# A four-slot graph network on one core: next inputs loaded early, and a new stage order on every engine

## What is computed

```
layer 0: A = exp(8*tanh((x q)(x k)^T / sqrt(128) / 8)) * adj, rows normalised; out = A x v
layer 1: x_h = elu(x Wi + bi); e = sigmoid(tgt_i + src_j + be) * mask; agg = e x_h
         out = [elu([agg, x_h * rowsum(e)] Wn + bn), x_h] Wm + bm
layer 2: Chebyshev terms I, L, 2LL-I of the normalised Laplacian; relu(sum_k T_k x W_k + b)
layer 3: 5 steps of a gated recurrence h -> (1-z)h + z*tanh(...), with adj*h in each gate
```

## Time and profile before

| | us |
|---|---|
| median of 3 runs | 2195.31 (2191.51 to 2196.2) |
| profiled execution, span | 2194.4 |
| VectorE busy | 1709.0 (78%) |
| ScalarE busy | 1182.5 (54%) |
| GpSimd busy | 1027.3 (47%) |
| mean granted TensorE clock | 0.952 of 2.4 GHz |

### The profile page before, as it was taken

One profiled execution on the slowest core, in us unless ns is written; L12 is line 12 of the kernel. 1 busy time (PEld: TensorE's weight loads), 2 busy tenths in 40 slices (PEclk: granted clock), 3 DMA queues, 4 the chain that ended last, 5 costly groups with the idle time before them and its releaser, 6 DMA issues.

```text
span 2194.4 us, 26908 instructions
## 1 busy us (share of the span) xinstructions
PE 1938.3 (88%) x8891; PEld 1418.6 (65%) x8891; DVE 1709.0 (78%) x3821; ACT 1182.5 (54%) x2177; POOL 1027.3 (47%) x812
## 2 busy tenths in 40 slices
...
GB/s 64 1 1 1 1 39 0 1 1 1 40 0 1 1 1 40 0 1 0 1 40 1 1 1 1 39 1 1 1 14 27 1 1 1 21 20 1 1 1 20
DMA packets 13512, 21.29 MB, mean 10 GB/s; under 512 B 2720, under 2 KB 5024, under 8 KB 13216
## 3 DMA queue, kind: packets, MB, share of 16 engines
...
q10 hardware_dynamic: 2576, 0.53, 0.1%
...
## 4 chain that ended last, share of the span: by engine, by line
PE 47%; DVE 29%; POOL 7%; ACT 7%; issue 6%; DMA 2%; SPq 0%; POOLq 0%; DVEq 0%; ACTq 0%
DVE X L696 5%; PE psA L1063 5%; PE psA L1064 5%; PE psB L890 4%; PE psB L892 3%; PE psB L891 3%; PE psA L885 3%; DVE H L848 3%; PE psA L1093 3%; DVE E L752 3%; DVE stat L675 3%; DVE E L844 2%; PE psA L890 2%; POOL rstd L390 2%; PE psA L891 2%
## 5 line engine op out<-in xcount | busy, mean ns | idle before, releaser
L425 POOL TENSOR_TENSOR S<-S,H 128x512 f32<-128x512 f32 x160 | 215.8, 1349 | 489.1 <-ACT S L562 489.1
L1063 PE MATMUL psA<-adjT_hi,nh_hi 128*128 128x512 f32 x640 | 273.7, 428 | 0.0
L1064 PE MATMUL psA<-adjT_hi,nh_lo 128*128 128x512 f32 x640 | 260.5, 407 | 0.0
L420 POOL TENSOR_TENSOR xT_lo<-H,xT_hi 128x512 fp32r<-128x512 f32 x160 | 240.4, 1510 | 32.8 <-ACT xT_hi L570 22.0
L381 POOL TENSOR_TENSOR S<-E 128x1024 f32<-128x1024 f32 x64 | 152.8, 2388 | 172.3 <-DVE E L710 119.1
L696 DVE TENSOR_SCALAR X<-X,mv,rstd 128x128 f32<-128x128 f32 x512 | 214.6, 482 | 16.2 <-POOL rstd L390 16.2
L388 POOL TENSOR_TENSOR rstd<-mv,eps_cols 128x4 f32<-128x4 f32 x128 | 49.3, 385 | 378.0 <-DVE mv L689 378.0
L844 DVE SCALAR_TENSOR_TENSOR E<-E 128x512 f32<-128x512 f32 x160 | 148.9, 931 | 95.3 <-ACT E L566 94.7
L665 DVE TENSOR_TENSOR nh_lo<-psA,nh_hi 128x512 fp32r<-128x512 f32 x128 | 88.0, 687 | 137.1 <-ACT nh_hi L575 137.1
L848 DVE SCALAR_TENSOR_TENSOR H<-E,S 128x512 f32<-128x512 f32 x160 | 165.2, 1032 | 9.3
L1093 PE MATMUL psA<-E,u5T 128*128 128x512 f32 x320 | 165.6, 599 | 0.0
...
## 6 DMA issues: line engine op xcount, KB each, us to landing
...
```

Source lines behind the costliest of these rows:

```text
L420: nc.gpsimd.tensor_tensor(xT_lo[s][:, :], H[s][:, :], xT_hi[s][:, :].bitcast(F32), ALU.subtract).then_inc(pool_done[s], 1)
L425: nc.gpsimd.tensor_tensor(kept[s], kept[s], H[s][:, :], ALU.mult).then_inc(pool_done[s], 1)
L1063: nc.tensor.matmul(psA[s][:, :], hi, adjT_hi[:, m, :], start=(m == 0), stop=False)
L1064: last = nc.tensor.matmul(psA[s][:, :], lo, adjT_hi[:, m, :], start=False, stop=(exact and m == TILES - 1))
```

## The change

The table of stages loses `load` and `store`, and nearly every number in it is another. SyncE's queue no longer comes from the table: it is a plain sequence of all loads and then all stores of a round, without a hardware loop. What a load waits for is the same count.

```diff
 SCHEDULE = [
-    ("load", 2.4, 0, 0, 0),
-    ("x0", 5.3, 10.4, 13.26, 0),
-    ("query", 4.5, 9.5, 12.6, 0),
+    ("x0", 4.56, 10.53, 11.19, 1.44),
+    ("query", 5.78, 12.46, 13.04, 9.75),
...
-    ("spread2", 9.53, 0, 9.5, 2.9),
-    ("norm2", 9.4, 0, 8.3, 0),
-    ("x3", 12.5, 2.5, 10.5, 0),
+    ("spread2", 52.78, 0.91, 10.44, 24.4),
+    ("norm2", 11.7, 1.48, 3.01, 1.11),
+    ("x3", 9.62, 8.59, 3.08, 3.66),
...
-    ("store", 4.8, 0, 0, 0),
 ]
-SLOT_LAG = 7.30
-PAIR_LAG = 14.28
+SLOT_LAG = 7.25
+PAIR_LAG = 14.32
...
-            stages = {"load": stage_load, "store": stage_store}
-            run("sync", stages, 0, first=True)
-            with sp.Fori(1, ROUNDS) as r:
-                run("sync", stages, r)
-            run("sync", stages, ROUNDS, last=True)
+            for r in range(ROUNDS):
+                for s in range(SLOTS):
+                    if r + 1 < ROUNDS:
+                        sp.wait_ge(residual[s], NORMS * r + 2)
+                        sp.dma_start(xin[s][:, :, :], xg[(r + 1) * SLOTS + s]).then_inc(loaded[s], 16)
+                for s in range(SLOTS):
+                    sp.wait_ge(normed[s], NORMS * (r + 1))
+                    sp.dma_start(og[r * SLOTS + s], X[s]).then_inc(stored[s], 16)
```

More of the change, by code:

```diff
@@ L41 @@
 SCHEDULE = [
-    ("load", 2.4, 0, 0, 0),
-    ("x0", 5.3, 10.4, 13.26, 0),
-    ("query", 4.5, 9.5, 12.6, 0),
-    ("scores01", 4.1, 10.4, 12.8, 0),
-    ("scores23", 5.5, 10.5, 11.4, 2.4),
-    ("mix", 2.7, 8.5, 0, 0),
-    ("out0", 0.77, 0, 0, 0),
-    ("sums0", 1.6, 0, 10.4, 0),
-    ("spread0", 1.9, 0, 11.7, 0),
-    ("norm0", 6.3, 0, 13.2, 0),
-    ("x1", 6.5, 7, 13.6, 0.1),
-    ("xh", 5.4, 7, 12, 0),
-    ("gates", 5.5, 0, 12.6, 0),
-    ("turn_xh", 6.7, 7.5, 11.1, 5.6),
-    ("agg", 8.37, 9.5, 13.5, 0),
@@ L57 @@
-    ("sums1", 2.33, 5.2, 11.3, 0.3),
-    ("recv", 1.67, 0, 0, 0),
-    ("self", 4.53, 10, 12.7, 0),
-    ("out1", 5.5, 0, 10.9, 0),
-    ("spread1", 2.63, 0, 8, 6.6),
-    ("norm1", 5.8, 0, 8.6, 0),
-    ("x2", 7, 10, 9.7, 0),
-    ("cheb01", 11, 10, 14.3, 0),
-    ("cheb23", 75.9, 10.3, 11, 3.4),
-    ("lap1", 14.8, 7.6, 13.1, 0),
-    ("lap_lo", 48.83, 0, 10.7, 0),
-    ("lap2", 10.5, 0, 10, 0),
-    ("spread2", 9.53, 0, 9.5, 2.9),
-    ("norm2", 9.4, 0, 8.3, 0),
-    ("x3", 12.5, 2.5, 10.5, 0),
@@ L104 @@
-    ("rh4", 1.2, 8.8, 13.1, 0),
-    ("split4", 3.16, 0, 0, 0),
-    ("t4", 0, 0, 0, 0),
-    ("last", 0, 0, 11.5, 0),
-    ("spread3", 5.13, 0, 12.72, 4.8),
-    ("norm3", 0.7, 0, 12.5, 0),
-    ("store", 4.8, 0, 0, 0),
+    ("x0", 4.56, 10.53, 11.19, 1.44),
+    ("query", 5.78, 12.46, 13.04, 9.75),
+    ("scores01", 5.26, 10.23, 12.76, 16.54),
+    ("scores23", 6.23, 11.42, 11.55, 0),
+    ("mix", 2.68, 10.41, 1.9, 6.77),
+    ("out0", 0, 10.78, 6.85, 6.17),
+    ("sums0", 2.17, 31.84, 11.37, 0.31),
@@ new lines @@
+    ("spread0", 1.24, 4.65, 10.7, 2.79),
+    ("norm0", 5.15, 0, 12.96, 0),
+    ("x1", 7.54, 10.88, 13.6, 3.65),
+    ("xh", 5.64, 10.76, 12.54, 6.49),
+    ("gates", 6.02, 0, 12.7, 8.19),
+    ("turn_xh", 5.92, 7.53, 10.72, 8.52),
+    ("agg", 9.39, 12.93, 14, 16.04),
+    ("sums1", 0, 0, 11.53, 0.37),
+    ("recv", 4.64, 0, 16.18, 13.36),
+    ("self", 5.94, 7.75, 10.25, 13.12),
+    ("out1", 5, 8.7, 11.16, 16.53),
+    ("spread1", 2.13, 1.91, 6.22, 0.86),
+    ("norm1", 3.54, 0.53, 8.77, 29.07),
```

84 lines of the change are left out of this document (44 added, 40 removed).

## The result

| | before | after |
|---|---|---|
| median, same chip | 2193.41 us (2190.44 to 2196.2, 4 runs) | 2145.47 us (2145.18 to 2147.64, 4 runs) |
| ratio | | 0.9782, 95% interval 0.9767 to 0.9796 |
| span of the profiled execution | 2194.4 us | 2143.9 us |

The change makes the kernel 2.2% faster, about 48 us. The forecast was 2173 with a range from 2148: right in direction, half of the gain, and the result lies 2.5 us outside the range.

What follows compares the result with a forecast made beforehand. Each round was taken as a VectorE phase joined to a TensorE phase (the recurrence) at seam and entry. 19.6 + 20.8 - 17.6 = 22.8 us off 2194.4, plus 0.9, gave 2172.5, say 2173 us; range 2148 to 2206.

Steps and rivals of the forecast that it cites:

- The loads: SyncE's queue and TensorE's input waits: earlier loads cost zero, VectorE having other work; bounds 3.1 us lost, 16.3 saved.
- Layer 1: Reorderings in layer 1 shorten waits for self.0, norm1.0 and self.3: +2.6 us a round, eight times, 20.8.
- The entry: Joint into the recurrence: two spreads ahead of norm2.0 start it later: -2.2 us a round, eight times, 17.6 lost.
- The seam: Joint where a round's last slots finish while the next round's slot 0 begins: +2.8 us, seven times, 19.6.
- (b): Round joint: norm3.3 loses its 3.1 us stretch beside GpSimd, spread3.3 gains one of 1.1: +2.0 us.
- (a): Round joint, loop turns: TensorE's gap now precedes x0.0, VectorE waits 2.5 us, less 0.8 for an earlier start: -1.7.
- over 5 us around x0.0, query.0 and x0.1: Sign that the forecast is wrong: VectorE waiting this long around these stages, where rounds join.
- The recurrence: Some 60 pairs swapped on TensorE and ScalarE: 0, TensorE being full, so gain excluded; bound -1 us per round.
- Nothing net: Rival, whole kernel: VectorE's work is the same, moved waits reappear elsewhere, 2191 to 2199 us; chance 0.13.
- The seam fails: Rival, round joint: VectorE waits 1.5 us more for each of three trips, 4.5 per joint, 2204 us; chance 0.24.
- The seam overlaps more: Rival: 1 us more gained per round joint, and start of recurrence costing only 0.8, 2155 us; chance 0.20.
- Rounds of 263: Sign that the forecast is right: length of a round after the change, in us.

Runs made afterwards that it cites:

- b_loads: Kernel before, old stage order, with only the new SyncE queue (all loads, then all stores): 2187.15 us, ratio 0.9983.

## Why the prediction was right or wrong

- **The loads.** "Cost zero", bounds 3.1 lost once and 16.3 saved: 3.7 us saved, inside the bounds. The reason given was half right: the waits of 3.1 us at x0.0 did reach the path in some rounds (seams of 44.8 and 45.2 us beside 40.3). The round of 266.2 us on which the forecast was worked out had only a short one (0.24 us).
- **Layer 1, +2.6 a round.** Right: 20.6 to 22.6 us against 20.8. By parts self.3 (0.6) and norm1.0 (0.40 and 2.17 to 1.36: 1.2) were hit; self.0's wait gave 0.5 of 0.8, and its instruction takes 0.5 more. The rest of the gain is not placed. The phase is 3.5 us shorter in the table, of which cheb01 to lap1.1 gives 0.7 back.
- **The entry, -2.2 a round.** Right in sign and near in size, but the 2.2 was hit by luck. The forecast was 1.6 for a later start and 0.6 for the clock. The start alone is 2.2 later: 1.6 by the remainder, as said, and 0.6 because ScalarE's copy of x3.0 then ends last, a path that the forecast left out. Undoing it gave 14 and not 17.6 over the kernel: the recurrence that starts 2.2 us earlier then takes 1.1 longer (107.1 against 106.0). The 0.6 for the clock had the wrong sign, for TensorE idles longer (8.89 us) and yet spends less time at half clock behind m0.0 (the clock of the 8.7 us behind it is 0.80, and 0.73 before); why, no run shows.
- **The seam, +2.8, seven times.** Wrong: in steady rounds 0.0 against the kernel before and -1.8 against b_loads, which has the same loads; over the kernel 8 to 11 us, nearly all in the first seam, where 19.6 were forecast. The terms that remove waits and the stretch held: norm3.3 4.23 to 1.10, and no wait at query.2, scores23.1 and query.3. Term (b) was short by one stretch: spread3.3 pays twice (0.92 and 1.17) and not 1.1 once. Here the Trainium skill (SBUF - State Buffer, Who interferes with whom), by whose turns "spread3.3 would meet both edge sums and pay twice", was nearer than my one stretch; the rest of that reading, 7 us, can't be picked out of the seam. The step that failed is (a), **-1.7**. Its gap was taken from the old place, 2.31 us, as a fixed price. In the new kernel it was 2.97, at most 3.8, with 4.3 us at half clock behind it, and VectorE waited 3.77 and then 1.35 more, not 2.5. That is 5.1 us, and "over 5 us around x0.0, query.0 and x0.1" was the forecast's own sign of being wrong. The Trainium skill (Runtime: NRT & Kernel Launch, Instruction fetch mechanics) was read in the forecast as "the gap follows the branch wherever it is put, at the same price". The rule itself makes the stall hang on whether the target's page is at hand, so on the place of the code, and the runs agree in that: moving the code took the loss from 2.9 to 4.0 us down to 0.2 to 1.3. That the stall is a fetch of code, no row shows. The same price everywhere was my addition, and wrong.
- **The recurrence, 0.** The step that put the result out of the range: "TensorE is full (1.0 us idle of 106.4) ..., so a gain is excluded". It gained 4.5 us a round, 30 us by the run that undoes it. The busy column was read as density. It covers a matmul's whole 0.40 us although the next could start after 0.23, so waits of up to about 0.2 us are inside "busy". The starts would have shown, before the change, six places in this round that are 0.16 to 0.83 us late, 2.1 us in sum, 17 in eight rounds: half of what the part brought, and enough to put the result inside the range. My bound, -1 us, reached to the other side only. The Trainium skill (Perfetto Trace Analysis, Identifying the Most-Contended Engine) says that the busy share of matmuls is no good measure of headroom, because they are pipelined, and to take the share of the weight loads, or of the peak in operations, instead. The trace agrees: by that column the recurrence stood at 81.37 of 110.3 us before, 74%, where the matmuls' column said 99%. I had not weighed that rule.
- **Rivals.** "Nothing net", where stretches "wander instead of going", was true in part: VectorE's norms and the three products of r and rh take 83 us less together, but the small TENSOR_SCALAR of the spreads (295 to 490 ns) and the one on U (775 to 972 ns) take 38 more. "The seam fails" priced three trips at 1.5 us more each; measured are 1.3 at x0.0 (3.77 against 2.5) and 1.35 in all behind it, 2.6 instead of 4.5. It was half true, and hidden under the recurrence's gain. "The seam overlaps more" was true for the first seam alone.
- **The sum.** By the ratios of the runs that undo a part, in us: loads 4, layer 1 23, seam 11, recurrence 30, entry -14, in sum 54 (parts that overlap); measured 48. The forecast's: 0, 20.8, 19.6, 0, -17.6. "Rounds of 263" came true (262.7) by luck: it was worked out from a round of the short kind (266.2, the mean is 268.4), whose seam then came out 2.0 us longer (40.3 to 42.3) and not 2.8 shorter, and the recurrence's 4.5 nearly cancel these 4.8.
